# Attention: the exponentials' sums go to the scores' banks in PSUM, and scores wait for the reciprocal

## What is computed

```
Q = (layernorm(x) @ Wq.T + bq)        # 4 x 16 heads x 2048 x 32
K, V = ctx @ Wk.T + bk, ctx @ Wv.T + bv   # 4 x 16 x 128 x 32
scores = Q @ K.T * 32**-0.5 / temperature
attn = softmax(scores, axis=-1)       # over the 128 keys
x = x + (attn @ V) @ Wo.T + bo
```

## Time and profile before

| | us |
|---|---|
| median of 3 runs | 1821.77 (1819.25 to 1824.95) |
| span of the profiled execution | 1821.3 |
| TensorE busy in the span | 1749.3 |
| VectorE busy | 1562.5 |
| ScalarE busy | 1226.0 |
| GpSimd busy | 972.2 |

### The profile page before, as it was taken

How to read it: one execution, slowest core, us unless ns; L and a number is a source line. 1 busy time by engine, 2 the same in 40 slices (tenths; PEclk the granted TensorE clock), 3 DMA queues, 4 the chain that set the end, 5 groups by cost and what they waited for, 6 DMA issues and landing times. The chain is left out here.

```text
span 1821.3 us, 29834 instructions
## 1 busy us (share of the span) xinstructions
PE 1749.3 (96%) x9082; PEld 1302.0 (71%) x9162; DVE 1562.5 (86%) x3587; ACT 1226.0 (67%) x3374; POOL 972.2 (53%) x1076
## 2 busy tenths in 40 slices
PE   8998799999999999999889999889999999999997
PEld 7776688888888888888634444357776776767765
DVE  6867799999999999988679888879888988888885
ACT  4675999999999999999542342356656655666543
POOL 2434466666666666666600000156766767767665
PEclk9999999999999999999989999999999999999999
DMA  8766445554455555544379999064545445445321
GB/s 306 222 218 164 115 124 140 152 153 139 137 158 153 141 141 155 153 116 118 98 259 390 402 394 370 26 229 161 173 150 193 164 153 197 157 159 170 124 58 41
DMA packets 153903, 322.08 MB, mean 177 GB/s; under 512 B 47377, under 2 KB 55569, under 8 KB 136081
## 3 DMA queue, kind: packets, MB, share of 16 engines
q1 hardware_dynamic: 153280, 319.38, 54.5%
q10 hardware_dynamic: 464, 0.79, 0.2%
HBM read 163.86 MB, written 105.91 MB: 148 GB/s over the span
## 5 line engine op out<-in xcount | busy, mean ns | idle before, releaser
L1306 POOL TENSOR_TENSOR a_pr<-a_pr,a_rcp 128x512 f32<-128x512 f32 x256 | 266.8, 1042 | 260.4 <-DVE a_rcp L1148 259.9
L1056 ACT ACTIVATE a_pr<-a_s,a_nmax 128x128 f32<-128x128 f32 x1024 | 366.4, 387 | 26.8 <-DVE a_nmax L1141 24.9
L1056 ACT ACTIVATION_READ_ACCUMULATOR a_pr<-a_s,a_nmax 128x1 f32 x1024 | 230.1, 225 | 0.0
L1561 PE MATMUL f_pair<-f_room,w 128*128 128x512 bf16 x999 | 225.0, 382 | 2.6 <-ACT f_room L1670 1.3
L1978 POOL TENSOR_TENSOR f_rs<-f_rs,f_half 128x1 f32<-128x1 f32 x128 | 121.4, 949 | 179.9 <-DVE f_rs L1825 179.9
L1779 DVE CUSTOM_DVE_ANT_0 f_hf<-f_pair,nb,sh 128x512 f32<-128x512 f32 x244 | 171.8, 748 | 30.7 <-PE f_pair L1561 23.2
L1561 PEld LDWEIGHTS f_pair<-f_room,w 128*128 128x128 bf16 x1024 | 99.5, 98 | 116.7 <-issue 3.6
L1156 DVE TENSOR_TENSOR a_pTl<-a_pt,a_pTh 128x512 fp32r<-128x512 f32 x256 | 168.6, 680 | 12.6 <-ACT a_pTh L1068 12.6
L1141 DVE TENSOR_REDUCE a_nmax<-a_s 128x4 f32<-128x512 f32 x256 | 172.1, 672 | 6.4 <-PE a_s L947 4.3
L959 PE MATMUL a_pt<-ident,a_pr 128*128 128x128 f32 x1024 | 160.9, 280 | 15.6 <-DVE a_pTl L1156 8.5
L1068 ACT ACTIVATE a_pTh<-a_pt 128x512 fp32r<-128x512 f32 x256 | 152.2, 630 | 2.8 <-PE a_pt L959 2.8
(11 more groups left out here) (442 smaller groups left out, 5055.8 us busy)
## 6 DMA issues: line engine op xcount, KB each, us to landing
hidden<-f_hf SPq DMA_DIRECT2D x57, 1024.0 KB, 9.4
f_hf<-hidden SPq DMA_DIRECT2D x57, 1024.0 KB, 4.8
xr<-x SPq DMA_DIRECT2D x96, 256.0 KB, 3.1
xb<-x SPq DMA_DIRECT2D x16, 1024.0 KB, 5.4
x<-xr SPq DMA_DIRECT2D x64, 256.0 KB, 2.3
ctxh<-bqreph SPq DMA_DIRECT2D x126, 128.0 KB, 2.4
f_room<-x SPq DMA_DIRECT2D x15, 1024.0 KB, 11.5
ctxh<-bqreph SPq DMA_DIRECT2D x128, 64.0 KB, 2.1
```

Source lines behind the costliest of these rows:

```text
L1056: last = e.activation(pr[:, t, j, :], s_bank[t][:, j * P:j * P + P], ACT.Exp, bias=nmax[kk % 2][:, t, j:j + 1], accum_out=sums[kk % 2][:, ...
L1306: e.tensor_tensor(p, p, rcp[kk % 2][:, t, :].unsqueeze(2).to_broadcast([P, 4, KEYS]), ALU.mult).then_inc(*e_pn)
L1561: last = e.matmul(h_bank[(PAIRS * u + i) % 3][:, q, :], w1[:, k, f * P:f * P + P], xT[u % 2][:, k, :], start=k == 0, stop=k == KC - 1)
```

## The change

`sums` is no longer a tensor in SBUF. It becomes a view of each slot's score bank: column 0 of each of the four heads, that is four elements 128 apart. When the sum of head j is written there, the exponentials of head j have read that column already. The reciprocal then reads its four sums out of PSUM. Since the bank now holds something that is wanted until the reciprocal has run, the scores (and the last outputs, which use the same banks) wait for `e_rc` in place of `e_exp`, with the same indices.

```diff
-        sums = [sb(f"sums{i}", [P, TPG, 4]) for i in range(2)]
+        sums = [bank[:].rearrange("p (j n) -> p j n", j=4)[:, :, 0] for bank in s_bank]
@@ scores, TensorE
-                e_exp.wait_ge(e, 4 * (u - 1) + (2, 1, 4, 3)[t])
+                e_rc.wait_ge(e, 4 * (u - 1) + (2, 1, 4, 3)[t])
@@ out, TensorE
                 if last_group(w):
-                    e_exp.wait_ge(e, 4 * NT - 1)
+                    e_rc.wait_ge(e, 4 * NT - 1)
@@ exp, ScalarE
                     last = e.activation(pr[:, t, j, :], s_bank[t][:, j * P:j * P + P], ACT.Exp,
-                                        bias=nmax[kk % 2][:, t, j:j + 1], accum_out=sums[kk % 2][:, t, j:j + 1])
+                                        bias=nmax[kk % 2][:, t, j:j + 1], accum_out=sums[t][:, j:j + 1])
@@ rc, VectorE
-                e.reciprocal(rcp[kk % 2][:, t, :], sums[kk % 2][:, t, :]).then_inc(*e_rc)
+                e.reciprocal(rcp[kk % 2][:, t, :], sums[t]).then_inc(*e_rc)
```

## The result

The changed kernel takes 1809.4 us (median of four runs, 1806.7 to 1811.9) against 1821.8 before (median of three; one more execution of that kernel took 7292 us and is left out). The ratio is 0.9934, with a 95% interval of 0.9919 to 0.9948: faster by 0.66%, or 12 us. A later measurement gave 1808.7 against 1819.3, a ratio of 0.9947 (0.9927 to 0.9967). The forecast was 1810.

What follows compares the result with a forecast made beforehand. The prediction took a closed loop of waits (11.24 us a step) as the bound, with PE's own 11.05 next; 62 x 0.19 = 11.8 us off the profiled span of 1821.3 gave 1809.5, put at 1810, range 1802 to 1824.

Steps and rivals of the forecast that it cites:

- The loop: Attention step: a closed chain of waits through ScalarE, VectorE and PE sets its 11.24 us; the change makes it 10.90.
- The hold of 0.05: ScalarE's sum reads: writing PSUM, each holds the engine 0.05 us in place of 0.09.
- Rival 1: ScalarE's sum reads: the hold stays 0.09, the engine's own time; about 1821 us, chance 0.32.
- rival 3: ScalarE: the exponential behind each sum read waits for its write to land; hold 0.19, 1890 us, chance 0.10.
- The reciprocal out of PSUM at nothing: VectorE's reciprocal: reading PSUM with stride 128 costs 0, with bounds of -0.02 and +0.06 us.
- Rival 2: VectorE: the saving comes but each reciprocal gets 0.06 us longer; 1814 us, chance 0.08.
- The scores' wait at nothing: PE's scores: waiting for the reciprocal instead of the exponentials costs 0; slot 2 is closest, with a margin of 0.55.
- rival 4: PE's slot 2 scores really wait for the reciprocal, 0.1 us a step; 1828 us, chance 0.04.
- Slot 3's 0.02: Slot 3's exponentials: only 0.02 us a step is free there before VectorE's own row is late itself.
- PE is late next: Attention step: with the loops shortened, PE's own pace of 11.05 us sets the step, which falls by 0.19.
- the second loop: From the reciprocal over GpSimd's product to slot 1's transposes and on through PE: 11.18 us, with 0.18 off 11.00.
- TensorE's two waits: PE in each step: 0.11 us of waiting in slot 1 and 0.06 before the values, taken as 0.19 with rounding.

Runs made afterwards that it cites:

- both edits that shortened it: Changed kernel with VectorE's slot 2 reciprocal ahead of x's low half: 1810.7 us; changed kernel with three small VectorE operations put a step later: 1813.5 us.

## Why the prediction was right, point by point

**The loop: right.** That a step is a closed loop which TensorE's 96% hides is what everything rested on. It passed the hardest test that I had: slot 1's reads, off the loop, give nothing, and those of slots 0 and 2 give all.

**The hold of 0.05: right.** It is 51 ns. Rival 1, that the hold is the engine's own time, is refuted, and so is rival 3: the next exponential doesn't wait for the landing (51 ns between the two, while the read lasts 160 to 310). The Trainium skill (Perfetto Trace Analysis, Optimizing Scalar/DVE Operations) had it about right, with its 93 and 51 ns beside 92 and 51 here.

**The reciprocal out of PSUM at nothing: right.** The changed kernel's reciprocals of slots 0 to 3 take 173, 167, 172 and 173 ns in the median, against 169, 164, 168 and 178 before, in spite of the stride of 128. Rival 2 is refuted, and with it the 0.065 estimated from the Trainium skill (VectorE: DVE Perf Modes, section on the TRN2 errata). The trace doesn't bear that rule out here.

**The scores' wait at nothing: right in its price, incomplete in its picture.** In the middle steps the margin in front of slot 2's scores is about 0.34 from the reciprocal's end to the weight load of the first of them. (The 0.55 of the prediction was up to the first product; up to its weight load it was 0.35 in the kernel before, too.) I had looked for rival 4 only there. It did come, in four steps of the opening with 1.2 more of waiting each, and it cost nothing, because TensorE had a wait of 1.74 to spend behind it. The run with the wait alone shows the same, 1.0007 (0.9995 to 1.0019).

**Slot 3's 0.02: right.** Alone it is worth 0 to 5 us by its interval; the step moved by 0.01.

**"PE is late next", at 11.05: this step failed.** The term that I mis-sized is the second loop: last reciprocal, GpSimd's product, transposes of slot 1, TensorE, the values, ScalarE's slot 2, x's copy, its low half, VectorE's row, last reciprocal. I took 0.18 off its 11.18 and had 11.00. Measured in medians it is 1.62 + 0.43 + 0.62 + 1.22 + 0.72 + 0.61 + 2.27 + 0.25 + 1.04 + 0.05 + 2.23 = 11.06, which but for rounding is the step of 11.07. The pieces are: first to last value product; the second value copy; slot 2's first exponential; x's copy; its low half; slot 2's reciprocal; slot 3's; the start of GpSimd's product; the product; the transposes' weights; the first value product. Of them 0.72 was 0.64 before: x's copy behind a sum read in PSUM takes 0.08 longer until its end. I had priced the sum read and the exponential behind it, and not the copy, the other thing that stands behind a sum read. The low half waits for a landing, and I had priced starts: from slot 2's first exponential to the low half the loop gains 2.03 - 1.94 = 0.09, where I had 0.16. So the second loop is what is late next. That GpSimd's product still ends 52 ns before the transposes' weights load (53 before) shows it closed, and TensorE still waits some 0.04 in slot 1 (0.844 in the median, 0.80 without waiting by the working on the earlier trace rows).

**The time: right, with a little luck.** The step fell by 0.17 and not by 0.19: 62 x 0.17 = 10.5 where I had 11.8. Besides, TensorE's two waits that I read, 0.11 and 0.06, add up to 0.17 and not to the 0.19 that I took "with rounding"; by 0.17 the forecast step would have been the measured 11.07, for a reason that did not hold. What made up for the difference: the last steps fell from 10.76 to 10.54, and the attention starts 0.9 earlier in the profiled execution, which may be chance. Another 2.8 of the 14.7 us between the two profiled spans lie behind the start of the last step and are in no term of mine. The difference to 1809.4 is far inside the 0.3% that can be told.

What was shown and what was argued: which slots pay, that the wait is free, that 0.04 of hold moves to a plain copy, that this copy's landing is on the loop, and that VectorE's row stands on it in half of the steps are shown by runs. Why the landings fall behind the starts isn't. That the second loop is the only one at 11.07 isn't: both edits that shortened it lengthened a neighbour in other steps, so no run shows the step with that loop alone relieved.

## What to carry to other kernels

When one engine shows 96% and the others 60 to 90%, take one period of the steady state and look for a closed chain of rows in which each starts right behind the one before. A saving counts if it lies on that chain, and only up to the length of the next chain, for which every instruction that stands behind the changed one has to be priced, too. Where the chain goes on from a landing, the landing is what has to be priced, and not the start. A new wait is best looked for in the opening and the end, where its cover is another; and a place that "has time" should be read in each kind of step, not in one.

## What the runs showed of the hardware beyond this

- A sum read of ScalarE (128x1) holds the engine 92 ns when it writes SBUF and 51 ns when it writes PSUM. In slots 0 and 2 the first of four reads lasts 164 and 163 ns in place of 193, but the durations grow by 18 or 19 from one to the next, where it was about 7: the fourth lasts 219 and 220 in place of 213 and 214. In slot 3 the fourth lasts 311 in place of 269. Over all 1024 the mean is 214 against 225.
- A plain copy out of PSUM (128x512) holds ScalarE 478 ns behind a read that wrote SBUF and 518 behind one that wrote PSUM; with a bias column it is 571 behind PSUM. In duration these are 610, 685 and 747.
- On VectorE the operation behind a 128-partition one of 512 elements starts some 0.60 after it, before that one has ended. Behind the addition that works on partitions 64 to 127 the next starts only 0.72 to 0.73 after it, once that has ended (444.45 to 445.18 above, and so in all 63 such places of the changed kernel with the reciprocal moved); behind its twin on partitions 0 to 63 after 0.60. That the partitions are the reason is not shown. This takes some 0.1 a step from VectorE's spare time (an estimate, 0.72 less 0.60). The twin in the changed kernel, and the operation behind it:

```profile
484.76 0.67 DVE L1179 TENSOR_TENSOR a_cs<-a_v,a_vl 64x512 f32<-64x512 f32 x1
485.36 0.67 DVE L1141 TENSOR_REDUCE a_nmax<-a_s 128x4 f32<-128x512 f32 x1
```
